# Attention passes in 64 by 64 parts of the array, and 640 instead of 768 first scores for a pair of heads, in a 16-batch transformer kernel

## What is computed

```python
x = x + 0.5 * L0_ffn(layernorm(x))        # gated, three layers of 512
x = x + L0_attn(layernorm(x))             # linear attention
x = x + 0.5 * L0_ffn(layernorm(x))
x = x + 0.5 * L1_ffn(layernorm(x))        # top 2 of 8 experts for each sequence
x = x + L1_attn(layernorm(x))
x = x + 0.5 * L1_ffn(layernorm(x))
...
scores = jnp.einsum('bhqd,bhkd->bhqk', q, k) * scale      # 16 heads of 8, with rope
scores = jnp.where(causal[None, None], scores, -jnp.inf)
attn = jax.nn.softmax(scores, axis=-1)
out = jnp.einsum('bhqk,bhkd->bhqd', attn, v)
```

## Time and profile before

| | |
|---|---|
| median of 3 runs | 648.39 us (647.62 to 648.92) |
| profiled execution: its time, its span | 650.77 us, 649.0 us |
| busy over the span: PE, DVE, ACT, POOL | 96%, 75%, 75%, 44% |
| mean granted TensorE clock | 0.989 |
| first passes run from, to | 412, 617 us |

### The profile page before, as it was taken

The page is one execution under the profiler, slowest core; times in us unless marked ns, Lnnn a source line. Parts: engine busy times, 40 slices in busy tenths (PEclk is TensorE's granted clock), DMA queues, the critical chain, the costliest instruction groups (busy, mean ns, idle before and its releaser), DMA issues.

```text
span 649.0 us, 14237 instructions
## 1 busy us (share of the span) xinstructions
PE 620.6 (96%) x5327; PEld 471.8 (73%) x5327; DVE 487.9 (75%) x1262; ACT 485.7 (75%) x816; POOL 287.1 (44%) x443
## 2 busy tenths in 40 slices
PE   4899999999999999999999999988999999999997
PEld 3777878888887887888778887756556666666675
DVE  6767566675766777665878767799998989989755
ACT  5789778787788787887888777624776668777882
POOL 1402303311311525223638354577787656656553
PEclk9899999999999999999999999999998989999999
DMA  9300000000000001100002025454354232231012
GB/s 292 107 2 1 0 1 2 1 2 1 1 1 2 0 2 49 49 1 1 1 26 66 8 82 163 155 175 139 103 150 144 72 103 91 68 112 53 4 36 67
DMA packets 41885, 37.79 MB, mean 58 GB/s; under 512 B 2940, under 2 KB 37020, under 8 KB 41816
## 3 DMA queue, kind: packets, MB, share of 16 engines
q1 hardware_dynamic: 41816, 36.87, 18.3%
HBM read 21.92 MB, written 14.68 MB: 56 GB/s over the span
## 4 chain that ended last, share of the span: by engine, by line
PE 70%; DVE 13%; ACT 9%; issue 6%; POOL 1%; DMA 0%; POOLq 0%; DVEq 0%; ACTq 0%
PE PSA L1015 20%; PE PSA L1019 19%; PE PSA L1252 7%; DVE MX L1439 5%; PE PSA L1228 3%; DVE G L1317 3%; PE PSA L1034 2%; PE PSA L1194 2%; ACT PSA L1486 2%; PE PSA L1171 2%; PE PSA L1178 2%; ACT G L1482 1%; PE PSA L1201 1%; PE PSA L1212 1%; PE PSA L1275 1%
## 5 line engine op out<-in xcount | busy, mean ns | idle before, releaser
L1015 PE MATMUL PSA<-ah,WH 128*128 128x512 f32 x320 | 130.0, 406 | 0.5 <-DVE G L1317 0.5
L1439 DVE TENSOR_REDUCE MX<-PSA 128x6 f32<-128x768 f32 x128 | 118.7, 951 | 13.5 <-PE PSA L1201 12.2
L1486 ACT ACTIVATE PSA<-PSA,SC 128x512 f32<-128x512 f32 x128 | 84.7, 662 | 55.0 <-PE PSA L1019 54.4
L1019 PE MATMUL PSA<-al,WH 128*128 128x512 f32 x320 | 125.2, 391 | 0.0
L1578 ACT ACTIVATE PB<-PSA 128x768 f32<-128x768 f32 x128 | 99.6, 812 | 30.8 <-PE PSA L1228 22.9
L1015 PE MATMUL PSA<-bh,WH 128*128 128x512 f32 x256 | 105.2, 411 | 2.7 <-DVE G L1317 2.3
L1019 PE MATMUL PSA<-bl,WH 128*128 128x512 f32 x256 | 100.2, 392 | 0.0
L1608 POOL TENSOR_SCALAR VE<-MV 128x4 f32<-128x4 f32 x46 | 11.4, 248 | 197.0 <-DVE MV L1292 197.0
L1322 DVE TENSOR_TENSOR al<-PSA,ah 128x512 fp32r<-128x512 f32 x64 | 44.0, 688 | 52.0 <-ACT ah L1493 51.6
L1668 POOL TENSOR_SCALAR_AFFINE_SELECT PB<-PB 128x512 f32<-128x512 f32 x95 | 60.4, 636 | 48.1 <-ACT PB L1578 46.4
L1322 DVE TENSOR_TENSOR bl<-PSA,bh 128x512 fp32r<-128x512 f32 x64 | 43.9, 687 | 34.8 <-ACT bh L1493 34.5
(11 more groups left out here) (165 smaller groups left out, 1302.2 us busy)
## 6 DMA issues: line engine op xcount, KB each, us to landing
KS<-dk SPq DMA_DIRECT2D x32, 192.0 KB
QS<-dq SPq DMA_DIRECT2D x32, 192.0 KB
dk<-CB SPq DMA_DIRECT2D x16, 192.0 KB, 2.3
dq<-CB SPq DMA_DIRECT2D x16, 192.0 KB, 2.5
VA<-in_ones SPq DMA_DIRECT2D x5, 512.0 KB, 5.1
X<-in_x SPq DMA_DIRECT2D x8, 256.0 KB, 6.8
dk<-CB SPq DMA_DIRECT2D x16, 128.0 KB, 2.1
dq<-CB SPq DMA_DIRECT2D x16, 128.0 KB, 1.9
```

Source lines behind the costliest of these rows:

```text
L1015: e.matmul(o, WH[:, col:col + 128], hi, start=first, stop=False)
L1019: return e.matmul(o, WH[:, col:col + 128], low, start=False, stop=last)
L1439: e.tensor_reduce(MX[:, u % 2, 1:4, :].rearrange("p t (l g) -> p l t g", l=2)[:, :, :, g], PSA[:, b:b + 2, 0:384].rearrange("p l (t k) -> ...
L1486: e.activation(bank(b), bank(b), ACT.Gelu, scale=SC[:, k:k + 1]).then_inc(a_gelu, 1)
```

## The change

Five edits:

- `pass1` works in four parts of 64 by 64 (two heads, two halves of output partitions). It takes the queries in blocks of 64: block 0 with 64 keys and block 1 with 128, then block 3 with 256 and block 2 with 192. Each partition so has 320 scores a head instead of 384, in five groups of 64. The mask takes four matmuls of 128 columns (before: four of 128 as well, but each on all 128 output partitions); in all it is 12 matmuls instead of 8.
- The tensor_reduce reads 640 elements and writes 10. `peak` on VectorE becomes three steps: a reduce over three groups, and two scalar_tensor_tensor that add the fourth group where it belongs, by the constant `CAP`. The second of them waits for the reduce.
- `max_out` becomes two ordinary matmuls, one of them with `ISB` (the identity with its halves swapped), and its result is float32, so VectorE copies 256 float32 elements.
- `pass2` makes the same columns in eight matmuls of 64 output partitions instead of four of 128. Of kind `m`, its mask takes four matmuls of 128 columns where it was four of 128 on all partitions; per row half it is 128 columns a part instead of 256.
- The planner's costs and `SHIFT` are others, so the order of all steps is another. 46 second passes are of kind `m` instead of 33, so there are 82 affine_selects on GpSimd instead of 95; 207 filling matmuls instead of 232; and in the planner's list TensorE changes its form 284 times instead of 301.

The diff, cut to its core:

```diff
-    "pass1": [("P", 0.29, 0.46), ("V", 0.868, 0.95)], "peak": [("V", 0.14, 0.22), ("A", 0.13, 0.24), ("G", 0.2, 0.26)],
+    "pass1": [("P", 0.225, 0.395), ("V", 0.735, 0.82)], "peak": [("V", 0.32, 0.4), ("A", 0.13, 0.24), ("G", 0.2, 0.26)],
...
 SHIFT = {
-    ("after", 0, 0): 0.67, ("after", 0, 2): -0.08, ("after", 0, 5): -0.22, ("after", 0, 6): 0.4,
+    ("after", 0, 0): -0.18, ("after", 0, 1): 0.71, ("after", 0, 6): -0.18, ("after", 0, 7): 0.13,
...
@@ tensor, pass1
-                    for k in range(2):
-
+                    for x in range(2):
                         for h in range(2):
-                            e.matmul(PSA[:, b + h, 0:384].rearrange("p (t k) -> p t k", t=3)[:, 0::2, 64 * k:64 * k + 64],
-                                     IM[64 * h:64 * h + 64, k, :], MK[64 * h:64 * h + 64, k, :, 64 * k:64 * k + 64],
-                                     start=(k == 0), stop=False, skip_group_check=True)
-                    for h in range(2):
-                        e.matmul(PSA[:, b + h, 0:128], Q[64 * h:64 * h + 50, g, 0:128], K[64 * h:64 * h + 50, g, 0:128],
-                                 start=False, stop=False, skip_group_check=True)
-                    for h in range(2):
-                        t = e.matmul(PSA[:, b + h, 128:384], Q[64 * h:64 * h + 50, g, 128:256],
-                                     K[64 * h:64 * h + 50, g, :], start=False, stop=True, skip_group_check=True)
+                            o = PSA[64 * x:64 * x + 64, b + h, 128:384] if x else PSA[0:64, b + h, 192:320]
+                            e.matmul(o.rearrange("p (t k) -> p t k", t=2)[:, :, 0:64], IM[64 * h:64 * h + 64, 0, 0:64],
+                                     MK[64 * h:64 * h + 64, 0, :, 0:64], start=True, stop=False, skip_group_check=True)
+
+                    for q, at in (((0, 1), (256, 192)), ((3, 2), (0, 0))):
+                        for x in range(2):
+                            for h in range(2):
+                                m = 64 * q[x] + 64
+                                t = e.matmul(PSA[64 * x:64 * x + 64, b + h, at[x]:at[x] + m], Q[64 * h:64 * h + 48, g, m - 64:m],
+                                             K[64 * h:64 * h + 48, g, 0:m], start=False, stop=True, skip_group_check=True)
@@ tensor, max_out
-                        t = e.transpose(T[:, 128 * k:128 * k + 128], HM[:, k, :, :].rearrange("p m h -> p (m h)"),
-                                        IDB[:, :])
+                        t = e.matmul(PSA[0:32, b, 128 * k:128 * k + 128], HM[:, k, :, :].rearrange("p m h -> p (m h)"),
+                                     ISB[:, :, :].rearrange("p t q -> p (t q)") if k else IDB[:, :], start=True, stop=True)
@@ tensor, pass2
                     for k in range(2):
+                        for x in range(2):
+                            for h in range(2):
+                                o = PSA[64 * x:64 * x + 64, b + h, 0:384].rearrange("p (t q) -> p t q", t=3)
+                                t = e.matmul(o[:, 1, :] if k else o[:, 0::2, :],
+                                             K[64 * h:64 * h + 52, g, 128 * k + 64 * x:128 * k + 64 * x + 64],
+                                             Q[64 * h:64 * h + 52, g, 128 * k:256], start=(k == 0), stop=not m,
+                                             skip_group_check=True)
...
@@ vector, pass1 and peak
-                    e.tensor_reduce(MX[:, u % 2, 1:4, :].rearrange("p t (l g) -> p l t g", l=2)[:, :, :, g],
-                                    PSA[:, b:b + 2, 0:384].rearrange("p l (t k) -> p l t k", t=3), AX,
+                    e.tensor_reduce(MX[:, u % 2, :, :].rearrange("p t (l g) -> p l t g", l=2)[:, :, :, g],
+                                    PSA[:, b:b + 2, 0:320].rearrange("p l (t k) -> p l t k", t=5), AX,
                                     ALU.max).then_inc(v_mx, 1)
...
-                    e.tensor_reduce(PK[:, u % 2, :, :], MX[:, u % 2, :, :].rearrange("p (q k) h -> p q h k", k=2), AX,
-                                    ALU.max).then_inc(v_peak, 1)
+                    e.tensor_reduce(PK[:, u % 2, 1, :], M[:, 0:3, :].rearrange("p k h -> p h k"), AX, ALU.max).then_inc(
+                        v_peak, 1)
+
+                    e.scalar_tensor_tensor(out=PK[:, u % 2, 0, :], in0=M[:, 3, :], scalar=CAP[:, 0:1], in1=M[:, 4, :],
+                                           op0=ALU.add, op1=ALU.max)
+                    w.wait_ge(v_peak, 2 * n + 1)
+                    e.scalar_tensor_tensor(out=PK[:, u % 2, 1, :], in0=M[:, 3, :], scalar=CAP[:, 1:2],
+                                           in1=PK[:, u % 2, 1, :], op0=ALU.add, op1=ALU.max).then_inc(v_peak, 1)
...
-                    e.tensor_copy(MT[:, u % 2, :], PSA[0:32, b, 0:128].bitcast(BF16)).then_inc(v_mt, 1)
+                    e.tensor_copy(MT[:, u % 2, :], PSA[0:32, b, 0:256]).then_inc(v_mt, 1)
```

More of the change, by code:

```diff
@@ new lines @@
+    ("after", 1, 0): -0.35, ("after", 1, 2): -0.45, ("after", 1, 4): 0.06, ("after", 1, 6): 0.35,
+    ("after", 1, 7): 0.01, ("attend", 0): -0.11, ("attend", 1): -0.45, ("attend", 2): -0.23, ("attend", 3): -0.02,
+    ("attend", 5): 0.41, ("attend", 6): 0.05, ("attend", 10): -0.14, ("attend", 11): 0.06, ("attend", 12): 0.15,
+    ("attend", 13): -0.25, ("ending", 0, 0): -0.15, ("ending", 0, 5): 0.25, ("ending", 1, 0): -0.03,
+    ("ending", 1, 3): -0.05, ("ending", 1, 6): -0.6, ("feed", 0, 1): 0.4, ("feed", 0, 3): -0.24,
@@ L130 @@
+    ("probs", 0): -0.08, ("probs", 2): -0.05, ("probs", 4): 0.14, ("probs", 6): 0.15, ("probs", 12): 0.03,
+    ("weigher", 2): -0.03, ("weigher", 4): -0.08, ("weigher", 5): 0.08, ("weigher", 6): 0.24,
+    ("weigher", 10): -0.25, ("weigher", 12): 0.17, ("weigher", 14): 0.04,
 }
@@ L771, in build @@
         IDB = sb("IDB", [128, 128], BF16)
+        ISB = sb("ISB", [128, 2, 64], BF16)
         IM = sb("IM", [128, 2, 128], BF16)
@@ L1224, in tensor @@
                     emptied(w, st.emptied)
+                    m = st.kind == "m"
                     for k in range(2):
-                        for h in range(2):
-                            o = PSA[:, b + h, 0:384].rearrange("p (t q) -> p t q", t=3)
-                            t = e.matmul(o[:, 1, :] if k else o[:, 0::2, :],
-                                         K[64 * h:64 * h + 52, g, 128 * k:128 * k + 128],
-                                         Q[64 * h:64 * h + 52, g, 128 * k:256], start=(k == 0), stop=st.kind != "m",
-                                         skip_group_check=True)
@@ L1232, in tensor @@
-                    if st.kind == "m":
-                        for k in range(2):
-                            for h in range(2):
-                                o = PSA[:, b + h, 0:256].rearrange("p (t q) -> p t q", t=2)
-                                t = e.matmul(o[:, :, 64 * k:64 * k + 64], MK[64 * h:64 * h + 64, k, 0, :],
-                                             IM[64 * h:64 * h + 64, k, 64 * k:64 * k + 64].rearrange(
-                                                 "p (o q) -> p o q", o=1).to_broadcast([64, 2, 64]),
-                                             start=False, stop=True, skip_group_check=True)
+                        for x in range(2):
[5 more added lines that the diff above has]
+                                             skip_group_check=True)
@@ new lines, in tensor @@
+                    for x in range(2 * m):
+                        for h in range(2):
+                            o = PSA[64 * x:64 * x + 64, b + h, 0:256].rearrange("p (t q) -> p t q", t=2)
+                            t = e.matmul(o[:, :, 64 * x:64 * x + 64], MK[64 * h:64 * h + 64, x, 0, 64 * x:64 * x + 64],
+                                         IM[64 * h:64 * h + 64, x, 64 * x:64 * x + 64].rearrange(
+                                             "p (o q) -> p o q", o=1).to_broadcast([64, 2, 64]),
+                                         start=False, stop=True, skip_group_check=True)
@@ L1279, in vector @@
         def vector(e, w):
+            for x in range(2):
+                for k in range(2):
+                    e.memset(CAP[64 * x:64 * x + 64, k:k + 1], -3.0e38 if x == k else 0.0).then_inc(v_cap, 1)
             for st in order.steps:
@@ L1627, in gpsimd @@
                     e.tensor_copy(IDB[:, :], IDN[:, :])
+                    for h in range(2):
+                        e.tensor_copy(ISB[:, h, :], IDN[:, 64 - 64 * h:128 - 64 * h])
                     w.wait_ge(s_rest, n_w4)
```

39 lines of the change are left out of this document (15 added, 24 removed), and 6 rows, old and new, of the table TAKES.

## The result

The change makes the kernel slower. The median of eleven executions is 653.23 us (650.89 to 655.17) against 648.39 before; the ratio is 1.0072 (95% interval 1.0057 to 1.0087), so +0.7% where -1.4% was forecast. The profiled execution took 653.23 us, span 651.5; before's took 650.77, span 649.0, both at a mean granted clock of 0.989.

The account below looks back on a forecast made before the run. TensorE and VectorE were both taken as near their limit from 412 to 617 us. Their sums, -9.3 and -12.0 us, were combined to -9.0: 648.4 - 9.0 = 639.4 us, forecast 636 to 643 (0.62), wider range 633.5 to 648.5.

Parts of the forecast that it names:

- The peak: VectorE's three small steps per peak: next instruction after 0.31 us instead of 0.13, +2.9 us for 16 sequences (+1 to +4.5).
- Both small things: The longer peak and the float32 copy for `max_out`, ahead of the second passes: their 0.3 us of delay is hidden.
- The text's own other branch: If second passes ran right behind the first, the delay of peak and copy would cost 16 x 0.3 = 5 us.
- How the two combine: TensorE's and VectorE's savings from 412 to 617 us: -10.3 us on the chain, taken as -9.0 us in all.
- TensorE's 9.3 us: TensorE's sum: first passes -8.3, second passes with masks +0.7, changes of form -1.7 us; between -13 and -3.
- The waits between the two do not shrink: Waits between TensorE and VectorE stay, so the gain was put at -9.0 us, a little under TensorE's own sum.
- The clock: Granted clock 0.92 from 500 to 550 us, up to 4 us another order may avoid: 635 us or less, chance 0.06.
- The new order: Changed costs and priorities move every wait from 412 us: half given back, about 644.5 us, chance 0.15; all, 648 us, 0.07.
- The named sign: If durations hold but the time doesn't fall, VectorE's waits for first passes should have grown above 12 us.
- The other one: Alternative sign that the order is to blame: the filling matmuls' time on TensorE should have grown.
- weight loads: Rival: column parts' loads queue within their row half on TensorE, 0.053 us each; 654.6 us, chance 0.07.
- column halves: Rival: on TensorE the two column halves don't run beside each other for bfloat16; about 681 us, chance 0.03.

Follow-up runs that it names:

- one-step: All new instructions in the order before, the peak one reduce over four of five part maxima (measures time, no valid replacement): 644.74 us, 0.9943 of the kernel before.
- one-max: All new instructions in the order before, one reduce over all five part maxima giving both rows of a partition the larger maximum: 647.55 us, 0.9966 of the kernel before.
- the filled wait and the short peak: The one-max kernel in the order before, plus 54 filling matmuls where TensorE waits for the first sequence's peaks: 645.70 us, 0.9944 of the kernel before.

## Why the prediction was wrong

Forecast was 639.4 us; it became 653.2.

- **Durations on TensorE and VectorE: right**, but for the peak. First pass 0.22 us (0.224 said), second 0.17 to 0.19 (0.184), loads, reduce, copy and changes of form as worked out.
- **The peak: mis-sized, and its delay wrongly called hidden.** The term was +2.9 us for VectorE, with 0.31 us until its next instruction and 0.40 from start to end. Unheld it is 0.41 us (436.07 to 436.48) and 0.48. In the change's profile it is 0.54 us from start to end on average, 8.6 us for 16 against 3.4, and in the old order 0.82, since more of the two-source steps are held behind GpSimd. The sentence that failed is "Both small things lie ahead of the second passes by whole sequences of first passes, so their 0.3 us of delay is hidden". The peak is followed by the negation, the transpose `max_out` and a copy, and these stand in line on TensorE and VectorE between first and second passes. The text's own other branch, 5 us if nothing hides it, was nearer: 6.4 and 6.3 us measured where the steps were taken out or put in, in the old order; 2.2 us in the change's own.
- **How the two combine: wrong.** I let TensorE's 9.3 us come through nearly whole. With a nearly as short peak as before's, the order kept and the clock at full, 5.8 us did; by the medians it was 3.9 (one-step) and 1.0 (one-max). "The waits between the two do not shrink" did not hold as said: in those two kernels TensorE's waits for a reduce to free banks did shrink (7.7 us before, 4.4 and 4.9), and VectorE's for first passes grew (17.4 and 14.9 us, before 12.2). Which of them takes the missing part, I have no run that isolates.
- **The clock** was mentioned only as a chance of gain. The change's mean clock was 0.988, before's 0.993 to 0.995. In before's own executions 0.011 of clock go with 3.7 us, so the 0.006 go with about 2 us, an estimate from those; it is part of the losses and not to be added. The two profiled executions, at the same 0.989, still lie 2.5 us apart.
- **The new order: the rival was right in kind and too small.** It was to give back half or all of the gain (0.22 together). By the ratios it costs 0.8 to 1.1% by itself in three pairs of kernels and 0.4% in the fourth, 2 to 7 us by the medians. The named sign was no sign: VectorE waits 15.1 us for first passes, above the 12.2, but it does so too in the kernels that became faster, and less in the old instructions' new order. The other one, the filling matmuls' time, fell, from 10.8 to 9.7 us. And the first passes, which should have ended some 8 us sooner, ended 0.9 us sooner; with the one-max peak in the old order it was 8.7 us (607.2 against 615.9), at a full clock.

From one measured kernel to the next, by medians against before: the forecast was -9.0 us; new instructions with the one-step peak in the old order gave -3.9; the three-step peak makes it +2.7, and the new order +4.8. By the other way, new instructions with the one-max peak in the old order gave -1.0, the new order makes it +2.5 and the three-step peak +4.8. So the shares of peak and order depend on which comes first: 6.6 and 2.1 us, or 2.3 and 3.5. No rival on the slower side named the peak. The 0.10 that I gave to "slower" rested on weight loads and column halves, which the trace then showed to be no matter.

## What to carry to other kernels

When two engines are near their limit, look for the small steps that connect them, and cost such a step by its whole way from the last input to the next engine's start, not by the busy time that it adds. A two-source VectorE instruction on SBUF data beside GpSimd work can last until GpSimd's instruction ends (up to 1.3 us here), so keep such steps off a chain that others wait for, or give them one source. An order that was searched anew has to be timed against the old order with the same instructions, and matmuls of neighbouring passes should be changed to a new form together, or each boundary between them priced (0.1 us here).

## What the runs showed of the hardware

- Nine of 32 scalar_tensor_tensor of 16 elements a partition took 0.33 to 1.31 us instead of 0.23 and ended within 0.04 us of a GpSimd instruction; no tensor_reduce with one source was touched, not even inside one (0.20 us at 462.38). A GpSimd power of 128x4 elements, 1.04 us, held none of the four that ran inside two of them.
- Matmuls of 48 to 64 rows by 64 columns on all four quarters of the array run side by side for bfloat16, 448 columns in 0.22 us, and their weight loads of 64 columns, 105 to 109 ns each, twelve in that pass, hide behind them.
- A tensor_reduce on 64 partitions is not short for it: 258 and 353 ns for 96 and 128 elements a partition, beside 210 and 280 for 64 and 80 on all partitions. No run has one shape on both.
- Changing TensorE's form costs 0.1 us: 0.38 against 0.29, 0.29 against 0.17 to 0.19, 0.33 against 0.22 and 0.27 against 0.17 us for a pass.
- The same program (`one_max_peak_old_order`) ran at mean clocks from 0.981 to 1.000, and its time from 649.8 to 641.1 us, shorter in the main at the higher clock. The kernels with all new instructions had mean clocks of 0.987 to 0.992 over their runs (0.994 with the filled wait and the short peak), the kernel before 0.993 to 0.995.
